# Weaving the last steps of two attention stages with the first steps of the next stage, with PSUM banks and SBUF areas reassigned

## What is computed

```python
h = concatenate([tokens(x), txt], axis=1)          # 128 x 96 x 64
h = h + gated_attention(ln(h))                     # stage a: square-relu kernel, rotary q and k, gate u
h = h + multihead_block(ln(h))                     # stage b: 4 heads x 4 query experts, causal softmax,
                                                   #   gated mix, layer norm, two 16x16 layers, softmax gate
h = h + rwkv_block(ln(h))                          # stage c: scan over tokens (exp, max), squared-relu layer
h = h + moe_top2(ln(h))                            # stages d, e: 64 experts, top 2
```

## Time and profile before

| | |
|---|---|
| median of 3 runs | 2512.23 us (2507.62 to 2513.51) |
| the profiled execution | 2496.42 us, of which the span of the trace is 2494.4 us |
| stage a ends, by the last `a_residual` | 439.4 us |
| stage b ends, by the last `b_w2` | 1461.2 us |
| busy share of the span | PE 77%, DVE 69%, POOL 41%, ACT 37% |
| mean granted clock of TensorE | 0.752 |

### The profile page before, as it was taken

The page is one execution under the profiler, slowest core; times in us unless marked ns, Lnnn a source line. Parts: engine busy times, 40 slices in busy tenths (PEclk is TensorE's granted clock), DMA queues, the critical chain, the costliest instruction groups (busy, mean ns, idle before and its releaser), DMA issues. The chain is left out here.

```text
span 2494.4 us, 51482 instructions
## 1 busy us (share of the span) xinstructions
PE 1922.1 (77%) x15831; PEld 1495.5 (60%) x15831; DVE 1715.0 (69%) x5200; ACT 919.3 (37%) x2958; POOL 1029.3 (41%) x878
## 2 busy tenths in 40 slices
PE   6888888799999999999999626777533332999970
PEld 2367767677777777777777414556422221887860
DVE  0069888358888888888888659999588883333223
ACT  2354343234444444444444238888422210111100
POOL 0023332013434434434443322222168875777772
PEclk9966676589999999999999656777755555555555
DMA  9900000000000000000000000000000002655526
GB/s 297 320 10 0 0 0 0 1 2 2 2 1 0 0 0 0 0 0 0 0 0 0 1 0 1 1 1 0 1 19 23 22 23 83 183 165 150 156 85 160
DMA packets 119880, 106.65 MB, mean 43 GB/s; under 512 B 62448, under 2 KB 109680, under 8 KB 118896
## 3 DMA queue, kind: packets, MB, share of 16 engines
q1 hardware_dynamic: 87024, 73.88, 11.0%
q10 hardware_dynamic: 18432, 16.79, 2.3%
q0 software_dynamic: 14336, 14.91, 1.8%
HBM read 78.84 MB, written 26.67 MB: 42 GB/s over the span
## 5 line engine op out<-in xcount | busy, mean ns | idle before, releaser
L988 ACT ACTIVATE arena<-PS 128x384 f32<-128x384 f32 (+3 forms) x384 | 178.3, 482 | 562.2 <-DMA arena<-in_t_experts_dram 216.5
L1336 POOL DMA_INDIRECT expert_rows<-arena x256 | 246.9, 965 | 104.4 <-issue 77.6
L1494 DVE TENSOR_REDUCE XR<-PS 128x2 f32<-128x192 f32 (+2 forms) x768 | 173.7, 280 | 107.4 <-PE PS L642 107.2
L642 PE MATMUL PS<-arena 32*128 32x96 f32 (+2 forms) x3072 | 235.0, 286 | 0.0
L1323 POOL DMA_INDIRECT routed_rows<-XR,SLu x192 | 199.8, 1041 | 74.9 <-issue 68.2
L642 PEld LDWEIGHTS PS<-arena 32*128 32x128 f32 x3072 | 199.1, 193 | 20.7
L1024 ACT ACTIVATE XR<-PS 128x256 f32<-128x256 f32 x512 | 167.3, 381 | 67.2 <-PE PS L657 67.0
L1277 POOL TENSOR_TENSOR arena<-arena,mhalf 96x16 f32<-96x16 f32 x32 | 92.7, 2896 | 225.8 <-DVE arena L1540 225.8
L1498 DVE TENSOR_TENSOR XR<-PS,XR 128x192 f32<-128x192 f32 (+2 forms) x768 | 172.4, 278 | 0.0
L609 PE MATMUL PS<-arena,WP 128*128 128x192 f32 x640 | 152.1, 363 | 18.4 <-ACT arena L988 17.8
L657 PE MATMUL PS<-WP,XR 128*128 128x128 f32 (+1 forms) x1024 | 163.7, 284 | 1.0 <-ACT XR L1024 1.0
(11 more groups left out here) (304 smaller groups left out, 4716.9 us busy)
## 6 DMA issues: line engine op xcount, KB each, us to landing
arena<-in_x_dram SPq DMA_DIRECT2D x32, 784.0 KB, 9.2
arena<-in_t_experts_dram ACTq DMA_DIRECT2D x128, 128.0 KB
arena<-in_t_experts_dram SPq DMA_DIRECT2D x128, 128.0 KB
routed_rows<-zt SPq DMA_DIRECT2D x16, 528.0 KB, 6.2
arena<-routed_rows SPq DMA_DIRECT2D x64, 132.0 KB
expert_rows<-arena POOLq DMA_INDIRECT x256
WP<-in_t_pack_dram SPq DMA_DIRECT2D x1, 3425.0 KB, 19.4
routed_rows<-XR,SLu POOLq DMA_INDIRECT x192, 2.2
```

Source lines behind the costliest of these rows:

```text
L642: mm = pe.matmul(PS[:, i, S_AT[j]:S_AT[j] + QB * (j + 1)], qF[rows, u, 3 * b + j, :], kF[rows, u, keys], start=False, stop=True, skip_grou ...
L988: return act.activation(dst, src, ACT.Identity, **kw)
L1336: pool.indirect_dma_start(YD, bass.IndirectOffsetOnAxis(yi[:, u % 4, k:k + 1], 0), yb[:, u % 4, k, :], None).then_inc(e_st[u % 2], 16)
L1494: dve.tensor_reduce(negmax[:, p, j, :], PS[:, 0:2, S_AT[j]:S_AT[j] + QB * (j + 1)], AX_X, ALU.max, negate=True).then_inc(b_max, 1)
```

## The change

At the seam a to b, DVE does the layer norm of the first groups of stage b between its last steps of stage a, and PE does step 0 of stage b ahead of its last step of stage a (`a_attend` and `a_output` of group 31). At the seam b to c, the tables and steps 0, 1 and 2 of stage c are written between the pieces of the last three steps of stage b, on each engine. The waits for the whole stage before give way to waits for single counts. The PSUM banks of stages b and c are renumbered and the SBUF areas moved, so that what two neighbouring stages use at the seam lies apart. No instruction of the computation is added or removed, and from step 3 of stage c on the order is as before.

The new helper, then TensorE at both seams:

```diff
+def part(n, t, *stages, unroll=2):
+    for lag, stage in stages:
+        if 0 <= t - lag < n:
+            stage(t - lag, (t - lag) % unroll)
...
-            grouped(pe, NG, (1, a_transpose), (3, a_attend), (1, a_projectB), (1, a_projectU), (2, a_scores), (3, a_output))
-            pe.wait_ge(a_h, NG)
+            grouped(pe, NG, *a_order, stop=NG + 2)
+            pe.wait_ge(ln_xF, NG)
+            pe.wait_ge(a_silu, 2 * NG)
...
-            T0_, O_, F_, Q_, Z_ = 2, 4, 5, 6, 7
+            F_, Q_, T0_, O_, S_, Z_ = 0, 1, 2, 4, 5, 7
...
+            part(NG, 0, *b_order)
+            part(NG, NG + 2, *a_order)
+            pe.wait_ge(a_h, NG)
+            grouped(pe, NG, *b_order, start=1, stop=NG + 1)
...
-            pe.wait_ge(b_h, NG)
-            T_, K_, V_, R_, OO, K0, K1, VV = range(8)
+            T_, K_, V_, R_, OO, K0, K1, VV = 0, 2, 3, 5, 4, 6, 7, 1
...
+            part(NG, NG + 2, *b_order[:fc1_at])
+            part(NR, 0, (0, c_transpose), unroll=4)
+            part(NG, NG + 2, *b_order[fc1_at:foT_at])
+            part(NR, 0, (0, c_kvr), unroll=4)
+            part(NG, NG + 2, *b_order[foT_at:])
+            part(NG, NG + 3, *b_order[:fc1_at])
+            part(NR, 1, (0, c_transpose), unroll=4)
+            part(NG, NG + 3, *b_order[fc1_at:foT_at])
+            pe.wait_ge(b_o, G * NG)
+            part(NR, 1, (0, c_kvr), (1, c_out), unroll=4)
```

ScalarE and GpSimd, second seam:

```diff
+            part(NR, 0, (0, c_squares), unroll=4)
+            part(NG, NG + 1, *b_order[foF_at:fxF_at])
+            part(NR, 0, (0, c_scale1), unroll=4)
...
+            part(NR, 1, (0, c_squares), (1, c_exps), unroll=4)
+            part(NG, NG + 2, *b_order[foF_at:wexp_at])
+            part(NR, 1, (0, c_scale1), unroll=4)
+            part(NG, NG + 2, *b_order[wexp_at:])
...
+            part(NG, NG + 3, *b_order[:weigh_at])
+            part(NR, 0, (0, c_power), unroll=4)
+            part(NG, NG + 3, *b_order[weigh_at:])
```

VectorE, first seam, and behind the dots the second (where the tables of stage c follow the wait for `b_h`):

```diff
+            dve.wait_ge(a_h, 4)
+            part(NG, 0, *b_order)
+            part(NG, NG + 1, *a_order)
+            part(NG, 1, *b_order)
+            part(NG, NG + 2, *a_order)
+            part(NG, NG + 3, *a_order)
+            dve.wait_ge(a_h, NG)
+            grouped(dve, NG, *b_order, start=2, stop=NG + 3)
...
-            dve.wait_ge(b_h, NG)
+            dve.wait_ge(b_h, NG - 3)
...
+            part(NR, 0, (0, c_ln), unroll=4)
+            part(NG, NG + 3, *b_order[:hn_at])
+            part(NR, 0, (0, c_var), unroll=4)
+            part(NG, NG + 3, *b_order[hn_at:h1_at])
+            part(NR, 0, (0, c_norm), unroll=4)
+            part(NG, NG + 3, *b_order[h1_at:])
+            part(NR, 1, (0, c_ln), unroll=4)
+            part(NG, NG + 4, *b_order[:fo_at])
+            part(NR, 1, (1, c_wkv1), unroll=4)
+            part(NG, NG + 4, *b_order[fo_at:hn_at])
+            part(NR, 1, (0, c_var), unroll=4)
+            part(NG, NG + 4, *b_order[hn_at:h1_at])
+            part(NR, 1, (0, c_norm), unroll=4)
+            part(NG, NG + 4, *b_order[h1_at:])
+            part(NR, 1, (1, c_wkv2), unroll=4)
+            part(NR, 2, (0, c_ln), unroll=4)
...
```

More of the change, by code:

```diff
@@ L65, in wait, with grouped @@
     eng.wait_ge(sem, value)
-def grouped(eng, n, *stages, unroll=2):
+def grouped(eng, n, *stages, unroll=2, start=0, stop=None):
     lmax = max(lag for lag, _ in stages)
@@ L78, in step @@
             stage(t - lag, (t - lag) % unroll)
-    for t in range(lo):
+    for t in range(start, lo):
         step(t, 0, n)
@@ L85, in grouped @@
                 stage(turn * unroll + (u - lag), (u - lag) % unroll)
-    for t in range(n, n + lmax):
+    for t in range(n, n + lmax if stop is None else stop):
         step(t, 0, n)
+def part(n, t, *stages, unroll=2):
+    for lag, stage in stages:
+        if 0 <= t - lag < n:
+            stage(t - lag, (t - lag) % unroll)
 class Link:
@@ L176, in build @@
         identb = tabs("identb", [P, P // 2]).bitcast(BF16)
-        t0, ta, tb, tc, td = (Arena(arena) for _ in range(5))
+        t0, ta, tb, tl, tc, td = (Arena(arena) for _ in range(6))
+        tb.at, tl.at = 8704, 16560
         ximg = t0("ximg", [RB, 4, G, 2, IMG])
@@ L838, in c_values @@
                 return stage
-            grouped(pe, NR, (4, c_values(0)), (4, c_values(1)), (3, c_transpose2), (3, c_mix(0)), (0, c_transpose), (0, c_kvr),
-                    (3, c_mix(1)), (1, c_out), unroll=4)
+            c_order = ((4, c_values(0)), (4, c_values(1)), (3, c_transpose2), (3, c_mix(0)), (0, c_transpose), (0, c_kvr),
+                    (3, c_mix(1)), (1, c_out))
+            fc1_at, foT_at = b_order.index((4, b_fc1s)), b_order.index((4, b_foTs))
+            part(NG, NG + 1, *b_order)
+            pe.wait_ge(b_vx, NG)
+            pe.wait_ge(b_pad, NG)
+            pe.wait_ge(b_exp, 4 * G * NG)
+            pe.wait_ge(b_sub, 6 * G * NG)
+            part(NG, NG + 2, *b_order[:fc1_at])
[8 more added lines that the diff above has]
+            part(NR, 1, (0, c_kvr), (1, c_out), unroll=4)
+            part(NG, NG + 3, *b_order[foT_at:])
+            part(NG, NG + 4, *b_order)
+            part(NR, 2, *c_order, unroll=4)
+            pe.wait_ge(b_h, NG)
+            grouped(pe, NR, *c_order, unroll=4, start=3)
             pe.wait_ge(c_h, NR)
@@ L1609, in b_w2 @@
                 dve.tensor_tensor(hgroup(g), hgroup(g), hsy[:, :], ALU.add).then_inc(b_h, 1)
[L1611 to L1612 removed]
+            b_order = ((6, b_var2), (5, b_var1), (4, b_outs(3)), (3, b_maxima(2, 1)), (6, b_fos), (3, b_maxima(3, 0)),
                     (0, b_ln), (3, b_outs(0)), (3, b_maxima(3, 1)), (6, b_w1), (5, b_hns), (2, b_padmask), (0, b_var),
@@ L1735, in c_end @@
                 dve.sem_inc(c_h, 1)
-            grouped(dve, NR, (0, c_ln), (1, c_wkv1), (3, c_norm2), (0, c_var), (2, c_resid), (4, c_end), (0, c_norm), (1, c_wkv2),
-                    (2, c_var2s), unroll=4)
+            c_order = ((0, c_ln), (1, c_wkv1), (3, c_norm2), (0, c_var), (2, c_resid), (4, c_end), (0, c_norm), (1, c_wkv2),
+                    (2, c_var2s))
+            fo_at, hn_at, h1_at = b_order.index((6, b_fos)), b_order.index((5, b_hns)), b_order.index((5, b_h1s))
+            part(NR, 0, (0, c_ln), unroll=4)
[6 more added lines that the diff above has]
+            part(NG, NG + 4, *b_order[:fo_at])
+            dve.wait_ge(b_om, G * NG)
+            part(NR, 1, (1, c_wkv1), unroll=4)
[6 more added lines that the diff above has]
+            part(NR, 2, (0, c_ln), unroll=4)
+            part(NG, NG + 5, *b_order[:fo_at])
+            part(NR, 2, (1, c_wkv1), unroll=4)
+            part(NG, NG + 5, *b_order[fo_at:hn_at])
+            part(NR, 2, (0, c_var), unroll=4)
+            part(NG, NG + 5, *b_order[hn_at:])
+            part(NR, 2, (2, c_resid), (0, c_norm), (1, c_wkv2), (2, c_var2s), unroll=4)
+            grouped(dve, NR, *c_order, unroll=4, start=3)
             dve.wait_ge(c_h, NR)
```

130 lines of the change are left out of this document (76 added, 54 removed).

## The result

| | before | after |
|---|---|---|
| median | 2509.93 us (4 runs, 2502.85 to 2513.51) | 2597.4 us (4 runs, 2592.11 to 2601.59) |
| ratio | | 1.0351, 95% interval 1.0324 to 1.0378 |
| span of the profiled execution | 2494.4 us | 2590.1 us |
| mean granted clock of TensorE | 0.752 | 0.712 |

The prediction was 2498 us and faster. The kernel became 3.5% slower, some 87 us. The ratios in this document are those of the runs in the fast state, and differ by up to 0.3% from the quotient of the medians beside them.

What follows compares the result with a forecast made beforehand. No engine was held busy throughout; DVE idled 41 of 96 us at the second seam, waiting on chains. First seam 0 and second seam -14 us, taken off the median, gave 2498 us, range 2485 to 2511.

Steps and rivals of the forecast that it cites:

- the last rival: Whole kernel: the change doesn't do what it says; held excluded by instruction order, with renumbered banks costing 0.
- a clock below 1.00 after 530: Stage b after 530 us: TensorE's granted clock under 1.00 there would show the prediction wrong.
- the rival of 8%: Entry to stage b: TensorE's clock rises later, each further low step costing 9 us, two giving 2516; chance 8%.
- First seam: Stage a to b: PE starts earlier but later waits take the gain back; 0 us, bounds -1.5 and +2.
- Second seam: Stage b to c: weaving fills part of DVE's 41 us of idleness; -14 us, bounds 7 and 20 of gain.
- items 1 and 2: Second seam: tables, `c_ln`, `c_norm` and `c_transpose` of group 0 go first; stage b late by 2.8, then 3.9 us.
- item 4: Second seam: `c_exps` of group 0 ahead of `b_foFs` of group 30 on ACT; late by 5.7 us.
- 5: Second seam: `b_w2` of group 30 waits for `b_wexp` behind `c_scale1` of group 1; late by 10.7 us.
- 6: Second seam: `b_w2`, `c_norm`, `c_transpose` precede `b_fc1s` of group 31, starting 1458.2; late by 12.4 us.
- 7: Second seam: `c_wkv2` of group 0 delays group 31; `b_fos` at 1477.5, `b_w2` ending 1483.1 instead of 1461.18.
- 8: Second seam: the rest of step 2 of stage c follows; `c_ln` of step 3 at 1494.5 instead of 1508.63.
- The rule on SBUF: Second seam: a skill page has two-input DVE and GpSimd instructions exclude each other; by it the seam would give 9 us.

Runs made afterwards that it cites:

- the first seam alone: Changed kernel with only the a-to-b seam woven, DVE's stage b loop in good place; against the kernel before 1.0025 without pad, 1.0024 with 108 idle instructions.
- +110: Changed kernel with 108 idle instructions more at DVE's start, stage b's loop 110 places on from the kernel before; ratio 0.995 to the kernel before.
- +66: Changed kernel with 64 idle instructions more at DVE's start, stage b's loop 66 places on from the kernel before; ratio 1.0203 to the kernel before.
- +2: Stage b's loop two places on in DVE's stream: kernel before with two idle instructions more, 1.0304; the changed kernel itself, 1.0351.
- +150: Kernel before with 150 idle instructions more at DVE's start; ratio 1.0333 to the kernel before.
- the long reduction: Kernel before with 108 idle instructions and one unread DVE reduction of about 3.5 us in each turn of stage b's loop; ratio 1.0478.

## Why the prediction was wrong, step by step

**The step that failed** is in the sum: "The change touches nothing that tells these apart, so I take the 14 off the median", and with it the last rival, "the renumbered banks carry the same instructions, and cost 0". That the banks cost nothing is right: with the first seam apart and banks and tiles as changed, the loop takes 721.2 us, against 722.0 before. But I took stage b's loop as a constant because its own instructions were the same. It has a term that neither its order nor its waits show, its place in DVE's stream, and this one was +96.5 us against a sum of -14. No rival had it. The two instructions that moved it were there to be counted.

**The clock.** The prediction held "a clock below 1.00 after 530" for a sign of error, and it was one, at both places. In the loop it followed DVE's stall. At the first seam it was the rival of 8%, "each further step at the low level costs 9"; the step cost 8.7, in four of seven profiles, so that 8% was too little. The reason against it was that PE's work from the first scores on is the same; that it is, and yet the clock fell again. The Trainium skill, page "TensorE: Matmul & The Clock Gate", section "Part 1: The HAM clock gate", was read as "a shorter idle gap at the seam can only help". PE's gap did shrink, from 5.44 us to 2.53, and the runs of the first seam alone, 1.0025 and 1.0024, show no help from it; their profiles have the long step. Which of PE's pauses decides between the two values stays open.

**First seam, predicted 0 (-1.5 to +2).** The walk was right up to the end of step 0 (452.45, or 454.1, where 454.2 was predicted). Then it took 4.7 us from `a_attend` to the end of the residual, which were 3.0 (452.29 to 455.31), so `b_maxima` comes 1.7 us ahead of the forecast, a little beyond the lower bound. With the clock's part the seam took 175.7 us on average over the seven woven profiles and 170.2 over the eight others, so the term is about +5.5.

**Second seam, predicted -14 (-7 to -20).** Right in size and at each item. With the loop in place it is 188.3 to 190.0 instead of 202.8, so -12.8 to -14.5; against the 204.2 that the eight profiles without this weave have on average, -14.2 to -15.9. The walk's own sums are off by some tenths: items 1 and 2 add up to 2.7 and 4.2 where 2.8 and 3.9 stand, the 1.4 us of item 4 are 1.6 by its rows, and at the first seam 458.9 goes on as 458.6. None moves a term by more than 0.4 us. The rows of the version +110, in which group 31 begins 0.6 us later than before, answer to the earlier trace rows; behind them ACT and POOL, to the earlier trace rows, and PE, to the earlier trace rows:

```profile
start us, us, engine line op out<-in xcount [idle before <-releaser]
1443.09 0.96 DVE L1748 TENSOR_TENSOR_SCAN arena<-arena 128x388 f32<-128x388 f32 x1
...
1455.27 0.17 DVE L1670 TENSOR_REDUCE arena<-arena 96x4 f32<-96x16 f32 x1 [4.94 <-ACT arena L1094]
...
1474.36 0.96 DVE L1748 TENSOR_TENSOR_SCAN arena<-arena 128x388 f32<-128x388 f32 x1
...
1478.04 0.42 DVE L1656 TENSOR_TENSOR arena<-arena 96x256 f32<-96x256 f32 x1 [1.54 <-POOL arena L1333]
...
1483.01 0.42 DVE L1675 TENSOR_TENSOR H<-H,arena 96x256 f32<-96x256 f32 x1
...
1494.75 0.67 DVE L1724 TENSOR_REDUCE arena<-H 96x8 f32<-96x512 f32 x1
```
```profile
1448.27 0.31 ACT L1021 ACTIVATE arena<-PS 128x192 f32<-128x192 f32 x1
...
1453.12 2.02 ACT L1021 ACTIVATE arena<-arena 96x64 f32<-96x64 f32 x8 [4.54 <-POOL arena L1348]
```
```profile
1442.73 2.90 POOL L1333 TENSOR_TENSOR arena<-arena,mhalf 96x16 f32<-96x16 f32 x1 [5.96 <-DVE arena L1606]
...
1450.08 3.00 POOL L1348 TENSOR_TENSOR arena<-arena,mhalf 96x16 f32<-96x16 f32 x1 [1.59 <-DVE arena L1732]
1474.52 3.48 POOL L1333 TENSOR_TENSOR arena<-arena,mhalf 96x16 f32<-96x16 f32 x1 [21.44 <-DVE arena L1606]
```
```profile
1458.12 0.90 PE L737 MATMUL PS<-arena,WP 128*128 128x192 f32 x2
```

| item | predicted us | measured us |
|---|---|---|
| 4: `b_foFs` of group 30 starts | 1448.35 | 1448.27 |
| 5: idle ahead of `b_w2` of group 30, ended by ACT | 4 to 5 | 4.94 |
| 5: `b_w2` of group 30 starts | 1455.2 | 1455.27 |
| 6: `b_fc1s` of group 31 starts | 1458.2 | 1458.12 |
| 7: `b_fos` of group 31 starts | 1477.5 | 1478.04 |
| 7: `b_w2` of group 31 ends | 1483.1 | 1483.43 |
| 8: `c_ln` of step 3 starts | 1494.5 | 1494.75 |

The costly place, `b_w2` of group 30 behind `b_wexp` behind `c_scale1` behind POOL's `c_power`, is where it was said to be. The measured times hold the 0.6 us of the later start, so that the walk is right to 0.7 us. In the changed kernel itself the seam gives less, 10.5, and 11.7 in the version +66; both have the loop out of place, and the reason for the difference is open. With the loop in place the whole change comes to 0.995 to 0.9995 of before, which is 2500 to 2511 us from the median that the prediction started from.

**The rule on SBUF.** `c_wkv1` (from 1443.09) runs inside POOL's power (1442.73 to 1445.63), and its scan took 0.96 us, as without a power beside it. So DVE does not wait out a power that began first, and the 9 us of gain by that rule were not the measurement. In the other order POOL takes longer: the power from 1474.52 began 0.16 us behind a scan and took 3.48 us instead of 2.90, and so it did (3.48 to 3.49) in all seven kernels with the second seam woven. The walk has 2.9 there, and these 0.58 us are about what it loses between items 6 and 7 of the table (0.62).

## What to carry to other kernels

When instructions are added ahead of a long loop, count where the loop comes to lie: one of 349 instructions on DVE may begin in 36 of each 128 places, and two waits too many cost 3.5% here. Only DVE's loop was moved here; of the other engines' no run tells. The signs of it in a profile are idle time that ends by "issue" at the top of each turn and packets of an instruction queue that recur with the loop; a pad of idle instructions in a stretch where the engine waits anyway tests it in one run, and repairs it. An unchanged stage belongs in the sum with a row from the trace after; until there is one, with a rival.

## What the runs showed of the hardware that was not expected

- DVE's instructions come in packets of 8,192 bytes (128 instructions), PE's in packets of 16,384 (some 255). DVE's loop of 349 runs without a fetch where it lies on three blocks of 128, and is fetched whole in every turn (five packets) where it lies on four, with a stall of 3.6 us at its top for +2 places and 2.4 for +66 and +150.
- A stall of 3.6 us on DVE in 57.7 us cost 4 us in an ordinary turn, and as much again on average because TensorE's granted clock fell to 0.50 for longer stretches in some turns (147 to 164 us of the loop in all, at +2 and with the long reduction); without the stall it stayed at 1.00 over all of the loop.
- Beside POOL's power DVE keeps its speed; beside a product of POOL it does not. In the version +110 the first instruction of `b_fos` took 0.53 to 0.94 us, half of the times over 0.88, in the 30 groups in which POOL ran its product of 96x256 beside it, and 0.42 and 0.43 in the other two. One of the 30:

```profile
1420.01 0.93 DVE L1656 TENSOR_TENSOR arena<-arena 96x256 f32<-96x256 f32 x1 [1.87 <-POOL arena L1333]
```
```profile
1419.95 1.58 POOL L1316 TENSOR_TENSOR arena<-arena 96x256 f32<-96x256 f32 x2
```

- Chips differ. On the two chips where the kernel before takes 2610 us, stages d and e took 807 to 810 us in the profiled executions, against 701 to 707 on the others, whatever the kernel; stage b's loop without the stall took 721.1 to 722.0 us on both kinds.
